# Attention queries as three products of high and low halves; the ring's zeros written by GpSimd; one buffer of normed rows

## What is computed

```python
x = layernorm(x + retention(x))          # layer 0, 16 heads with decay
x = layernorm(x + ternary_ffn(x))        # layer 0, weights -1/0/1, 1024 hidden
x = layernorm(x + attention(x))          # layer 1, see below
x = layernorm(x + mixture_of_experts(x)) # layer 1, 8 experts, top 2, capacity 160
# attention(x), cut to its start:
xn = x * rsqrt(mean(x * x) + eps) * g1
Q, K, V = xn @ Wq.T, xn @ Wk.T, xn @ Wv.T
pQ, pK = elu(Q), elu(K)                  # then per-token mixing of the 16 heads
```

## Time and profile before

| | us |
|---|---|
| median of 3 runs | 890.84 (890.45 to 896.16) |
| the profiled execution | 892.54 |
| its span | 890.9 |
| PE busy / DVE busy / ACT busy / POOL busy | 815.3 / 598.5 / 488.7 / 272.7 |
| mean granted TensorE clock | 0.977 |

### The profile page before, as it was taken

One profiled execution on the slowest core, in us unless ns is written; L12 is line 12 of the kernel. 1 busy time (PEld: TensorE's weight loads), 2 busy tenths in 40 slices (PEclk: granted clock), 3 DMA queues, 4 the chain that ended last, 5 costly groups with the idle time before them and its releaser, 6 DMA issues. The chain is left out here.

```text
span 890.9 us, 23450 instructions
## 1 busy us (share of the span) xinstructions
PE 815.3 (92%) x8950; PEld 667.5 (75%) x8950; DVE 598.5 (67%) x1439; ACT 488.7 (55%) x1018; POOL 272.7 (31%) x335
## 2 busy tenths in 40 slices
PE   6999999998899999998999899998988879999960
PEld 5888888887677777766777688886655549999950
DVE  3677778778557777778555425577667886657627
ACT  2544443443777777775974244556575435454426
POOL 1257763221112222224000000124443134656344
PEclk9999999999999999999999999999999989999985
DMA  8600000000000000001478534435222314566439
GB/s 321 197 21 22 18 24 18 18 12 3 1 1 1 1 1 1 1 1 34 126 196 199 132 92 131 136 101 198 93 85 99 103 31 121 142 201 161 119 64 343
DMA packets 74637, 79.55 MB, mean 89 GB/s; under 512 B 21824, under 2 KB 65728, under 8 KB 74176
## 3 DMA queue, kind: packets, MB, share of 16 engines
q1 hardware_dynamic: 69584, 72.36, 26.6%
q0 software_dynamic: 3968, 5.25, 3.4%
q10 hardware_dynamic: 1008, 0.91, 0.3%
HBM read 50.70 MB, written 27.79 MB: 88 GB/s over the span
## 5 line engine op out<-in xcount | busy, mean ns | idle before, releaser
L729 DVE TENSOR_TENSOR r_prob<-r_pS,const 128x512 f32<-128x512 f32 x128 | 81.9, 682 | 24.7 <-PE r_pS L551 24.7
L1106 DVE SCALAR_TENSOR_TENSOR f_gl<-att_res,small_first,f_gh 128x512 fp32r<-128x512 f32 x64 | 47.3, 747 | 35.7 <-ACT f_gh L1031 33.4
L1685 POOL TENSOR_TENSOR att_res<-att_res,t_hy 128x1024 f32<-128x1024 f32 x8 | 15.5, 1958 | 165.2 <-DVEq L2182 165.2
L960 PE MATMUL f_pY<-wpjT,f_gh 128*128 128x256 f32 x256 | 65.4, 290 | 0.3 <-DVE f_gl L1106 0.3
L961 PE MATMUL f_pY<-wpjT,f_gl 128*128 128x256 f32 x256 | 62.7, 279 | 0.0
L1374 PEld LDWEIGHTS q_bank<-q_xT,att_res 128*64 128x64 f32 x1024 | 57.3, 140 | 7.2 <-issue 4.2
L1374 PE MATMUL q_bank<-q_xT,att_res 128*64 128x128 f32 x1024 | 60.9, 279 | 0.0
L960 PEld LDWEIGHTS f_pY<-wpjT,f_gh 128*128 128x128 f32 x256 | 48.1, 188 | 15.9 <-issue 13.4
L2595 POOL DMA_INDIRECT sum_dram<-e_yo,y_id x24 | 43.1, 1795 | 54.6 <-ACT e_yo L2732 39.5
L1025 ACT ACTIVATE att_res<-f_pH 128x512 f32<-128x512 f32 x64 | 38.0, 594 | 38.6 <-PE f_pH L945 37.8
L2713 ACT ACTIVATE e_hh<-e_pH 128x320 fp32r<-128x320 f32 x64 | 26.2, 433 | 54.0 <-PE e_pH L2637 53.8
(11 more groups left out here) (336 smaller groups left out, 2350.6 us busy)
## 6 DMA issues: line engine op xcount, KB each, us to landing
kv_dram<-att_res SPq DMA_DIRECT2D x32, 256.0 KB, 3.5
t_ring<-kv_dram SPq DMA_DIRECT2D x128, 64.0 KB, 2.3
wi<-L_ffn_wi SPq DMA_DIRECT2D x8, 1024.0 KB, 5.0
wo<-L_ffn_wo SPq DMA_DIRECT2D x8, 1024.0 KB, 7.6
x_res<-L_attn_x SPq DMA_DIRECT2D x8, 512.0 KB, 7.0
q_dram<-att_res SPq DMA_DIRECT2D x16, 256.0 KB, 3.5
t_q<-q_dram SPq DMA_DIRECT2D x8, 512.0 KB, 4.4
x_dram<-x_res SPq DMA_DIRECT2D x8, 512.0 KB, 3.0
```

The costliest lines, as they stand in the source:

```text
L729: dve.tensor_tensor(prob[t % 2][:, r, :, :], pS[r][:, :, :], dec[:, r, :, :], ALU.mult)\
L960: pe.matmul(out, gh[c % 4][:, cols], net.wpjT[:, c, :], start=(c == 0 and t % 2 == 0), stop=False, skip_group_check=True)
L1106: dve.scalar_tensor_tensor(out=gl[c % 4][:, :], in0=g[c][:, :], scalar=net.lnw[:, c:c + 1], in1=gh[c % 4][:, :], op0=ALU.mult, op1=ALU.sub ...
```

## The change

Queries are computed as xh*wqh + xl*wqh + xh*wql, all in fp32r: xh and wqh are rows and weights rounded to fp32r, xl and wql the rests. So items 0 and 1 have six products each in place of two f32 ones. ACT writes xh beside xT in `take`; DVE makes xl in a new step `low`, behind item 3 of the batch before, and for batch 0 behind the making of `qscale`. Of xh and xl there is one buffer each. The weights are split in batch 2 of the feed-forward: one ACT copy and one DVE subtraction. PE's `body` and `front` wait for the new semaphore x_split too. xn has one buffer in place of two; the second rl buffer moves into a free part of att_res. The zeros of the ring are written by POOL in 48 memsets of 512 columns, behind its work for the feed-forward, and ACT has no `clear` any more.

```diff
# ternary_ffn, scalar, batch 2
+                if b == 2 and c == 1:
+                    act.wait_ge(net.later_in.sem, net.later_in.after(48))
+                    nc.scalar.activation(net.wqh[:, :, :], net.wqkvT[:, :, 0:DIM], ACT.Copy)
# ternary_ffn, vector, called at b == 2 and c == 3
+        def low_weights():
+            dve.wait_ge(sums_kept.sem, sums_kept.after(2))
+            dve.tensor_tensor(net.wql[:, :, :], net.wqkvT[:, :, 0:DIM], net.wqh[:, :, :], ALU.subtract)
# attention_inputs
-    xn = [ph.sb(f"xn{i}", [P, TPB, DIM]) for i in two]
+    xn = ph.sb("xn", [P, TPB, DIM])
-    rl = [ph.sb(f"rl{i}", [P, SEQ]) for i in two]
+    rl = [ph.sb("rl0", [P, SEQ]), spare[:, 6 * KD * SEQ:6 * KD * SEQ + SEQ]]
+    xh, xl = (ph.sb(n, [P, KD, SEQ], F32R) for n in ("xh", "xl"))
+    net.wqh, net.wql = (ph.sb(n, [P, KD, DIM], F32R) for n in ("wqh", "wql"))
+    def gpsimd(pool):
+        pool.wait_ge(net.x_ready.sem, net.x_ready.after(BATCH))
+        pool.wait_ge(net.q_rs_ready.sem, net.q_rs_ready.after(BATCH))
+        for r in range(RING):
+            dst = net.ring[r][:, :, :].rearrange("p c n -> p (c n)")
+            n = dst.shape[1] // 16
+            for part in range(16):
+                ins = pool.memset(dst[:, part * n:(part + 1) * n], 0.0)
+                if part % 4 == 3:
+                    ins.then_inc(net.ring_zeroed.sem, 1)
# scalar: take (clear and its place between the batches are removed)
             for k in range(KD):
-                ins = nc.scalar.activation(xT[p][:, k, :], pX[k][:, :], ACT.Copy, scale=g1[:, k:k + 1])
-            ins.then_inc(xT_ready.sem, 1)
+                nc.scalar.activation(xh[:, k, :], pX[k][:, :], ACT.Copy, scale=g1[:, k:k + 1])
+                nc.scalar.activation(xT[p][:, k, :], pX[k][:, :], ACT.Copy, scale=g1[:, k:k + 1]).then_inc(xT_ready.sem, 1)
# tensor: body
-            pe.wait_ge(xT_ready.sem, xT_ready.after(b + 1))
+            pe.wait_ge(xT_ready.sem, xT_ready.after(2 * b + 2))
+            pe.wait_ge(x_split.sem, x_split.after(b + 1))
...
-                    for k in range(KD):
-                        mm = pe.matmul(out[:, :], net.wqkvT[:, k, n * P:(n + 1) * P], xT[p][:, k, :], start=(k == 0), stop=(k == KD - 1))
+                    terms = [(w, x, k) for k in range(KD) for w, x in ((net.wqh, xh), (net.wqh, xl), (net.wql, xh))]
+                    for m, (w, x, k) in enumerate(terms):
+                        mm = pe.matmul(out[:, :], w[:, k, n * P:(n + 1) * P], x[:, k, :], start=(m == 0), stop=(m == len(terms) - 1))
# vector
+        def low(b, p):
+            for k in range(KD):
+                dve.wait_ge(xT_ready.sem, xT_ready.after(2 * b + k + 1))
+                ins = dve.tensor_tensor(xl[:, k, :], xT[p][:, k, :], xh[:, k, :], ALU.subtract)
+            ins.then_inc(x_split.sem, 1)
 # norm
-            if not isinstance(b, int) or b >= 2:
-                dve.wait_ge(turned.sem, turned.after(b - 1))
+            if not isinstance(b, int) or b:
+                dve.wait_ge(turned.sem, turned.after(b))
 # body
+                if n == 3 and behind:
+                    low(b + 1, 1 - p)
 # first, behind the making of qscale
+            low(0, 0)
             batches(dve, body, steps, 4, first=last_norm)
```

More of the change, by code:

```diff
@@ L1214, in vector @@
                     low(b + 1, (c - 3) // 3)
+                if b == 2 and c == 3:
+                    low_weights()
                 if b and c == 3:
@@ L1271, in attention_inputs @@
     lam_ready, exp_lam = (ph.sig(n) for n in ("lam_ready", "exp_lam"))
-    xn_ready, turned, xT_ready = (ph.sig(n) for n in ("xn_ready", "turned", "xT_ready"))
+    xn_ready, turned, x_split = (ph.sig(n) for n in ("xn_ready", "turned", "x_split"))
+    xT_ready = ph.sig("xT_ready")
     e_made, e_taken, v_made = ph.sig("e_made"), ph.sig("e_taken", 4), ph.sig("v_made")
@@ L1276, in attention_inputs @@
     stored = net.stored
-    step, nothing_ready = ph.sig("step"), ph.sig("nothing_ready")
-    nothing = ph.sb("nothing", [P, 1])
+    step = ph.sig("step")
     ITEMS = 3 * KD
@@ L1325, in body @@
                 take(b + 1, 1 - p)
[L1327 to L1332, removed]
         def first():
@@ L1340, in rest @@
             nc.scalar.activation(lmb[:, 2:4], lmb[:, 0:2], ACT.Exp).then_inc(exp_lam.sem, 1)
[L1341 to L1350, removed]
+            for b in range(BATCH):
+                body(b, b % 2, b > 0, b < BATCH - 1)
         return first, rest
@@ L1359, in front @@
             else:
-                pe.wait_ge(xT_ready.sem, xT_ready.after(b))
+                pe.wait_ge(xT_ready.sem, xT_ready.after(2 * b))
+                pe.wait_ge(x_split.sem, x_split.after(b))
             for k in range(KD):
                 for t in range(TPB):
-                    mm = pe.transpose(pX[k][:, t * P:(t + 1) * P], xn[p][:, t, k * P:(k + 1) * P], net.table["ident"])
+                    mm = pe.transpose(pX[k][:, t * P:(t + 1) * P], xn[:, t, k * P:(k + 1) * P], net.table["ident"])
             mm.then_inc(turned.sem, 1)
@@ L1418, in set_up @@
             dve.tensor_tensor(lmb[:, 0:2], lv[:, :, 0], lv[:, :, 1], ALU.mult).then_inc(lam_ready.sem, 1)
-            dve.memset(nothing[:, :], 0.0).then_inc(nothing_ready.sem, 1)
+        def low(b, p):
[3 more added lines that the diff above has]
+            ins.then_inc(x_split.sem, 1)
         def norm(b, p):
             dve.wait_ge(net.q_rs_ready.sem, net.q_rs_ready.after(b + 1))
-            if not isinstance(b, int) or b >= 2:
-                dve.wait_ge(turned.sem, turned.after(b - 1))
-                dve.sem_inc(net.passed, 1)
+            if not isinstance(b, int) or b:
+                dve.wait_ge(turned.sem, turned.after(b))
             for t in range(TPB):
-                ins = dve.tensor_scalar(xn[p][:, t, :], tile_of(net, b * TPB + t), net.q_rs[:, bass.ds(b * TPB + t, 1)], None, ALU.mult)
+                ins = dve.tensor_scalar(xn[:, t, :], tile_of(net, b * TPB + t), net.q_rs[:, bass.ds(b * TPB + t, 1)], None, ALU.mult)
             ins.then_inc(xn_ready.sem, 1)
@@ L1463, in first @@
             dve.wait_ge(steps.sem, steps.done(1))
+            low(0, 0)
             batches(dve, body, steps, 4, first=last_norm)
         return set_up, norm, first
-    return sync, scalar, tensor, vector
+    return sync, gpsimd, scalar, tensor, vector
 def first_layer_and_inputs(net, ctx):
@@ L1483, in first_layer_and_inputs @@
     f_gpsimd, f_scalar, f_tensor, f_vector = of_ffn
-    q_sync, q_scalar, q_tensor, q_vector = of_inputs
+    q_sync, q_gpsimd, q_scalar, q_tensor, q_vector = of_inputs
     nc.all_engine_barrier()
@@ L1497, in _ @@
         f_gpsimd(pool)
+        q_gpsimd(pool)
     @block.scalar
```

## The result

| | before | after |
|---|---|---|
| median of the runs taken side by side, us | 894.42 (11 runs, 890.45 to 896.16) | 898.49 (11 runs, 893.67 to 901.42) |
| the profiled execution, us | 892.54 | 898.25 |
| its span, us | 890.9 | 896.5 |
| PE / DVE / ACT / POOL busy, us | 815.3 / 598.5 / 488.7 / 272.7 | 811.7 / 613.2 / 477.9 / 298.6 |
| mean granted TensorE clock | 0.977 | 0.971 |

The ratio is 1.0039 [1.0023, 1.0054]: 3.5 us slower, 2.1 to 4.8. The forecast of +2.5 us lies in that interval. Its time, 893.3, does not match: it was put on 890.84, the median of three runs, and with eleven runs the kernel before takes 894.42. The measured 898.49 lies above the top of the range, 897.0.

The account below looks back on a forecast made before the run. PE, almost without a gap, was taken to bound the stage: +5.1 (start) + 2.2 (clock) - 4.3 (products) - 0.8 (ACT) + 0.3 (feed-forward) = +2.5 us, 890.84 to 893.3, range 889.5 to 897.0.

Parts of the forecast that it names:

- the last of the sum: Whole kernel: +2.5 us put on the median of three runs, 890.84, giving 893.3; on the profiled execution it gave 895.0.
- The products: Items 0 and 1 of each batch: twelve fp32r products take 3.01 us in place of 3.63, gain 0.62 a batch.
- The start: Batch 0: PE waits for the first split behind DVE's queue, starting at about 415.2 in place of 405.63; +5.1 us.
- The clock: Start of batch 0: after the long idle time PE resumes at half clock, costing 2.2 us, ends 1.7 and 3.4.
- ACT and the zeros: Early batches: batch 3 no longer waits for ACT; POOL's zeros end at 449 to 450, or some 457, cost 0.
- The 0.8: Batch 3's late start on ACT, which clears the ring ahead of it, goes away: 0.8 us gained.
- `low`: Batches 1 to 7: DVE's split ends before PE wants it, with 0.4 us of cover, and costs nothing.
- Rival (2): Batches 1 to 7: low isn't hidden; 0.3 us late makes it +4.6, 895.5; chance 10%.
- The feed-forward's 0.3: Feed-forward: one ACT copy and one DVE subtraction to split the weights cost 0 to 0.7 us, taken as 0.3.
- Behind the stage "nothing changes": After the stage: no cost, since the next phase starts when SP has issued the last stores, which moves with PE.
- The bounds: Whole change: the terms' ends sum to -0.1 us at best, with 0.4 for no border in batch 0, +4.9 at worst.

Follow-up runs that it names:

- plain_first: Changed kernel, but batch 0 takes its queries from the f32 products of the kernel before, without the split: 892.3 beside 894.71 for the kernel before, ratio 0.9974.
- split_early: Changed kernel, but DVE makes the first split ahead of the last feed-forward rows: 892.98 beside 894.71 for the kernel before, ratio 0.9988 [0.9965, 1.001].
- before_again: The kernel before, unedited, as a control: 895.67 beside 893.87, ratio 1.0002 [0.9982, 1.0021].
- zeros_only: Kernel before with only the zeros changed, POOL's 48 memsets in place of ACT's clear: 892.0 beside 894.71, ratio 0.9968 [0.9943, 0.9992].
- changed_again: The changed kernel, unedited, measured again: 898.42 beside 894.67 for the kernel before, ratio 1.0037 [1.0022, 1.0052].
- clock_kept: Changed kernel with eleven idle products on PE while it waits for the first split: 899.59 beside 894.71 for the kernel before, ratio 1.0055.
- clock_kept_9: Changed kernel with nine idle products on PE while it waits for the first split: 895.0 beside 894.67 for the kernel before, ratio 1.0002.

## Where the prediction failed, and what in it was right

**The step that failed** is the last of the sum, the level that the change was added to: "against the median, 890.84 becomes 893.3. The profiled execution stands 1.7 us above the median, so I give the second". That median was of three runs which spread over 5.7 us (890.45, 890.84 and 896.16). The kernel before takes 894.42 in the median of eleven, and 893.9 to 896.6 in the other medians of 12 to 35. Two of the three runs were of its rarest kind: of the 108 others only 6 took less than 891 us. So 3.6 of the 5.2 us between 893.3 and 898.49 are the level; the same +2.5 on 894.42 gives 896.9, and the range moved by as much would end at 900.6. I let the top of the range carry the scatter of the level with half a sentence, when it was larger than all bounds of the terms; from the execution shown, +2.5 gave 895.0, the better number.

The other 1.6 us are the change itself: the medians differ by 4.1 in place of 2.5 (3.5 [2.1, 4.8] by the ratio). Its sign was right, and the mechanism inside the stage. That +2.5 falls into the interval is in part luck, for the terms inside the stage were forecast to give 2.2 and gave 1.7, the 0.3 of the feed-forward can't be seen, and some 1.7 us come from outside the stage, which the forecast had at nothing. Step by step:

- **The products.** Forecast 0.62 us a batch, 11.3 from batch to batch; measured 0.68 and 11.26. Items 0 and 1 take 2.95, not 3.01: the borders between the kinds cost a little less.
- **The start.** Item 0 was forecast at 415.2 and came at 415.80, of which 0.53 was there at the first transposes already. plain_first and split_early, which take that wait away or shorten it, by two different ways, have stages 4.2 and 4.7 us shorter than the changed kernel. That is less than the 7.3 of start and clock together, since `low(1)` then waits for DVE in its turn (2.73 and 2.06 us). In the changed kernel that second wait isn't there, as the prediction said of `front(1)`; it shows only once the first is gone.
- **The clock.** Forecast 2.2; items 0 and 1 took 5.15 in place of 2.95, 2.20. The forecast's ends were 1.7 and 3.4, so that it met the first decimal is luck. From the first transposes to batch 1: forecast +7.3, measured +7.32.
- **ACT and the zeros.** The wait of 0.77 us is gone, and the memsets ran from 424.74 to 451.15 with no one waiting. I named the batch wrongly: the late one is batch 4, the fifth; its `take`, made in `body(3)`, stands behind the last four zero instructions. The 0.8 was right against that execution but not the whole of what ACT cost. I took the clock fall of the earlier trace rows for a cost that PE bears, and the 0.77 for all that ACT costs. before_again shows that ACT sets batch 4's start in either case, so that fall and wait are one sum, 2.44 = 1.67 + 0.77; zeros_only, with neither, is 2.5 shorter.
- **`low`.** Its cost is 0, as forecast, but with 0.22 us of cover in place of 0.4. Where the difference goes, I didn't measure. Rival (2), that `low` isn't hidden, was nearer than its price said.
- **The feed-forward's 0.3** isn't seen. Among the eight executions without a clock fall ahead of the stage, the latest start of it is 403.76, and that is zeros_only, which doesn't split the weights; the six with the split start at 403.44 to 403.71, the kernel before at 403.18. So the 0.53 ahead of the stage isn't shown to be the split's.
- **Behind the stage "nothing changes".** Not shown wrong and not shown right. From PE's first product of the next phase to its last one that reads m_hot (the experts' selection, near the end of that phase) it was 221.1 and 223.2 us in two executions of the kernel before, 223.8 twice in the changed one. The 2.1 us between the first two are mostly one clock fall, so the excess is 2.8 against the one and 0.6 against the other.
- **The bounds.** The best sum has a slip: by the costs that it charges, leaving out the border cost in batch 0 is worth 0.2, not 0.4, so the best is +0.1. It changes nothing in the range. The other sums come out to within 0.1.

**Open.** The measured change is 1.7 us more than the stage's, at both measurements. One candidate is the clock fall near 620 to 630, behind a gap of about 2.7 us in PE's work that both kernels have. It is there in both profiled executions of the changed kernel and in one of two of the kernel before, and costs 1.4 to 1.7. Whether the changed kernel meets it more often, two executions each don't show. The listed clocks only bound it: 0.9688 in the mean of changed_again, 0.9763 in the mean of the 30 executions beside it, 6.7 us of clock over 897. The fall in the stage alone (half clock from about 407.0 to 420.6, against 3.4 us or nothing before) makes 5.2 to 6.9 of them, which leaves nothing to 1.6 us for falls elsewhere. So they could carry most of the difference, or none. Why the executions of clock_kept have more falls than those of clock_kept_9 is open too.

## What to carry to other kernels

A cheaper operation that needs one more step on another engine pays that step's place in the hand-written order once, at the first batch; here 0.68 us in each of the seven later batches and 0.84 of ACT's wait didn't pay for a batch 1 that starts 7.3 us later. Let the first batch use the old form, and then look for the wait that the first one had covered. A wait of 0.8 us can be the visible end of a chain that bounds several batches: add up what the engine does from one fixed point to the next before pricing its relief. And take the level from as many runs as the answer needs; three were 3.6 us off here. When runs of one kernel differ, compare their granted clocks and look for the clock falls ahead of the stage before blaming the change.

## What the runs showed of the hardware

- A memset on POOL slows a one-input scaling of DVE with its input in SBUF: norm's four instructions took 2.26 to 2.54 us beside the memsets (2.49 in the row above) and 1.13 to 1.14 without, 557 ns an instruction in zeros_only against 349 in the kernel before. In the terms of the sum I had counted only the 0.43 us scalings as touched. The memsets themselves were hardly held up: 26.4 us for 48, where 0.53 each made 25. DVE's instruction with two inputs kept its 0.69 us. The Trainium skill (SBUF — State Buffer, "Who interferes with whom") says a two-port DVE instruction and one of GpSimd exclude each other, and that one with two inputs contends only with GpSimd reading. Both agree with these rows.
- The same gap in PE's work is followed by a fall of the granted clock from 1.00 to 0.50 (2.4 to 1.2 GHz) in one execution and not in the next. The 2.1 us ahead of the transposes of batch 1 were followed by 64 products of 5.38 us in the first execution of the kernel before, and of 3.71 in the second and in zeros_only. The 2.7 us near 620 have a fall in 8 of the 14 profiled executions. The price is 1.4 to 1.7 us each time.
